# Log-distances from one product per head, and ScalarE writing two of four heads in the cross-attention

## The reference, cut to what matters

```python
log_fg = jax.nn.log_sigmoid(f_pre)
lf_cs = jnp.cumsum(log_fg, axis=-1)
...
log_d = lf[..., 1:, None] - lf[..., None, 1:] + i_pre[..., None, :]
log_d = jnp.where(mask, log_d, -jnp.inf)
m = jnp.max(log_d, axis=-1, keepdims=True)
d_mat = jnp.exp(log_d - m)
scores = jnp.einsum('bhtd,bhsd->bhts', q, k) * (1.0 / np.sqrt(DH))
s_mat = scores * d_mat
denom = jnp.maximum(jnp.abs(jnp.sum(s_mat, axis=-1, keepdims=True)), jnp.exp(-m)) + BACKEND_EPS
return jnp.einsum('bhts,bhsd->bhtd', s_mat, v) / denom
```

```python
def stablemax(x):
    s = jnp.where(x >= 0, x + 1.0, 1.0 / (1.0 - x))
    return s / jnp.sum(s, axis=-1, keepdims=True)
```

## Time and profile before

| what | value |
|---|---|
| median of three runs | 3640.21 us |
| profiled execution, its own time | 3634.66 us |
| span of its records | 3633.0 us |
| PE busy over the span | 2876.1 us (79%) |
| DVE busy | 2268.1 us (62%) |
| ACT busy | 1511.0 us (42%) |
| POOL busy | 667.5 us (18%) |

### The profile page before, as it was taken

One profiled execution on the slowest core, in us unless ns is written; L12 is line 12 of the kernel. 1 busy time (PEld: TensorE's weight loads), 2 busy tenths in 40 slices (PEclk: granted clock), 3 DMA queues, 4 the chain that ended last, 5 costly groups with the idle time before them and its releaser, 6 DMA issues. The chain is left out here.

```text
span 3633.0 us, 60719 instructions
## 1 busy us (share of the span) xinstructions
PE 2876.1 (79%) x21702; PEld 2244.0 (62%) x21703; DVE 2268.1 (62%) x3977; ACT 1511.0 (42%) x2470; POOL 667.5 (18%) x640
## 2 busy tenths in 40 slices
PE   4999877777655699999206999879999999177796
PEld 3666555555445588888205888756666666166686
DVE  5554557777644211111456888879999999778542
ACT  1233244434311122222004666568888888178000
POOL 0111103333346201001570000021111110000600
PEclk9999988888855799999658999889999999699898
DMA  3000051111132444444230000000000000034444
GB/s 110 0 0 0 20 205 53 53 53 53 36 123 96 151 145 141 145 142 141 86 102 27 1 1 1 1 31 13 13 13 13 13 13 7 25 162 185 173 150 162
DMA packets 109948, 259.90 MB, mean 72 GB/s; under 512 B 15040, under 2 KB 52928, under 8 KB 101056
## 3 DMA queue, kind: packets, MB, share of 16 engines
q1 hardware_dynamic: 91712, 204.85, 16.4%
q0 software_dynamic: 18048, 52.45, 4.4%
HBM read 169.17 MB, written 88.08 MB: 71 GB/s over the span
## 5 line engine op out<-in xcount | busy, mean ns | idle before, releaser
L1765 DVE TENSOR_SCALAR e_low<-bank 128x2048 f32<-128x2048 f32 x128 | 293.1, 2290 | 37.1 <-PE bank L1637 34.0
L1159 ACT ACTIVATE cx_h<-bank,c_b 128x256 f32<-128x256 f32 x288 | 120.7, 470 | 409.6 <-PE bank L1114 409.6
L1114 PE MATMUL bank<-cx_zT,cx_w 128*128 128x256 f32 x1152 | 262.5, 381 | 1.8 <-DMA cx_w<-cw_dram 0.9
L1125 PE MATMUL bank<-c_w,cx_h 128*128 x1152 | 260.4, 379 | 0.0
L1589 ACT ACTIVATE e_low<-e_low 128x2048 f32<-128x2048 f32 x128 | 245.1, 1915 | 2.1
L1586 ACT ACTIVATE e_low<-e_low 128x2048 f32<-128x2048 f32 x128 | 243.5, 1903 | 0.0
L1114 PEld LDWEIGHTS bank<-cx_zT,cx_w 128*128 128x128 f32 x1152 | 220.3, 191 | 32.3 <-DMA cx_w<-cw_dram 1.3
L2131 PE MATMUL bank<-f_wout,fd_q 128*128 128x256 f32 x1024 | 224.2, 383 | 19.6 <-DVE fd_q L2150 19.6
L1125 PEld LDWEIGHTS bank<-c_w,cx_h 128*128 128x128 f32 x1152 | 213.6, 190 | 25.9
L2131 PEld LDWEIGHTS bank<-f_wout,fd_q 128*128 128x128 f32 x1024 | 196.7, 192 | 46.9 <-DVE fd_q L2150 19.8
L1766 DVE TENSOR_SCALAR e_high<-bank 128x1536 f32<-128x1536 f32 x128 | 223.8, 1749 | 0.0
(11 more groups left out here) (362 smaller groups left out, 6781.9 us busy)
## 6 DMA issues: line engine op xcount, KB each, us to landing
cx_w<-cw_dram SPq DMA_DIRECT2D x72, 512.0 KB, 3.2
hidden<-fu_h SPq DMA_DIRECT2D x32, 1024.0 KB, 3.9
fd_h<-hidden SPq DMA_DIRECT2D x32, 1024.0 KB, 4.8
cx_rows<-expert_rows SPq DMA_DIRECT2D x72, 256.0 KB, 3.2
slot_y<-cx_y POOLq DMA_DIRECT2D x72, 256.0 KB, 2.5
X<-x_dram SPq DMA_DIRECT2D x4, 2048.0 KB, 16.0
g_cT<-ctxT_dram SPq DMA_DIRECT2D x32, 256.0 KB, 5.4
queries<-g_qT SPq DMA_DIRECT2D x32, 256.0 KB, 6.2
```

The lines of the kernel that those rows point to most:

```text
L1114: last = nc.tensor.matmul(H[k][f // 2][:, (f % 2) * GROUP_ROWS:(f % 2 + 1) * GROUP_ROWS], w1[k][:, c, f * P:(f + 1) * P], zT[k][:, c, :], ...
L1125: last = nc.tensor.matmul(Y[k][:, n * D:(n + 1) * D], h[k][:, f, n * P:(n + 1) * P], w2[:, bass.ds(e, 1), f, :].rearrange("p o d -> p (o d ...
L1159: nc.scalar.activation(h[k][:, f, :], H[k][f // 2][:, (f % 2) * GROUP_ROWS:(f % 2 + 1) * GROUP_ROWS], ACT.Gelu, bias=b1[:, bass.ds(e, 1), ...
L1765: nc.vector.tensor_scalar(flat(low[n % RING][:]), HEADS4.rearrange("p r s -> p (r s)"), -1.0, 0.0, ALU.mult, ALU.max).then_inc(neg_ready, 1)
```

## The change

**Recurrent attention.** The log-distance g[s] - top[t] is taken apart. g[s] is constant over a row of the tile (sources lie on the partitions), so it no longer goes through the product: PE turns gg once a group (own_term), ACT copies it to gT, and the exponential takes it as its bias. Since the bias differs between the two halves of the sources, the exponential of a head is two instructions, of 256 and of 128 columns. -top[t] comes from one product: a constant bf16 table minus of -1 in a head's three rows, filled in the gate stage by four copies, times top3, which holds the three bf16 parts of top. The mask stays a product. lefts and rights go, and part 1 and part 2 of prepare change. The three column blocks are now stored so that the first 256 columns are the first half of the sources and the last 128 the second half; scores and values keep their column counts.

**Cross-attention.** DVE writes high of heads 0 and 1, ACT of heads 2 and 3.

```diff
-LEFT1, LEFT1C, LEFT2, LEFT2C = (4 + 4 * k for k in range(4))
-RIGHT1, RIGHT1C, RIGHT2, RIGHT2C = (20 + 8 * k for k in range(4))
...
-            table = lambda at, n: s["rows"][:, at:at + n]
-            nc.vector.tensor_copy(table(BLOCK01, 2), ends[:])
-            nc.vector.tensor_tensor(table(EVEN, 1), low[:, 0:1], high[:, 0:1], ALU.add)
-            nc.vector.scalar_tensor_tensor(table(ODD, 1), low[:, 1:2], -1.0, high[:, 1:2], ALU.mult, ALU.subtract)
-            nc.vector.tensor_scalar(table(LEFT1, LANES4), lane[:], ends[:, 0:1], None, ALU.mult)
-            nc.vector.tensor_scalar(table(LEFT1C, LANES4), lane[:], ends[:, 1:2], -1.0, ALU.mult, ALU.mult)
-            nc.vector.tensor_scalar(table(LEFT2, LANES4), lane[:], low[:, 0:1], None, ALU.mult)
-            nc.vector.tensor_scalar(table(LEFT2C, LANES4), lane[:], high[:, 0:1], -1.0, ALU.mult, ALU.mult)
-            nc.vector.tensor_tensor(table(RIGHT1, HEADS), high[:, 2:2 + HEADS], high[:, 2 + HEADS:2 + 2 * HEADS], ALU.add)
...
+            nc.vector.tensor_copy(s["part"][:, 0:1], low[:, 0:1])
+            nc.vector.tensor_scalar(s["part"][:, 1:2], low[:, 1:2], -1.0, None, ALU.mult)
+            nc.vector.tensor_copy(s["part"][:, 2:3], high[:, 0:1])
+            nc.vector.tensor_tensor(heads[:], low[:, 2:2 + HEADS], low[:, 2 + HEADS:2 + 2 * HEADS], ALU.add).then_inc(rows_ready, 1)
+            dve.wait_ge(rows_ready, 1)
+            nc.vector.tensor_tensor(heads[:], heads[:], high[:, 2 + HEADS:2 + 2 * HEADS], ALU.add).then_inc(rows_ready, 1)
+            dve.wait_ge(rows_ready, 2)
+            for j in LANES:
+                nc.vector.tensor_scalar(which[:, j, :], heads[:], lane[:, j:j + 1], -1.0, ALU.mult, ALU.mult).then_inc(rows_ready, 1)
...
+                if g < LANES4:
+                    nc.vector.tensor_copy(s["minus"][:, g], which[:, g, :, None].to_broadcast([P, HEADS, P]))
...
         soft, cum, gg, top, gm = (sb(n, [P, S]) for n in ("soft", "cum", "gg", "top", "gm"))
-        x0, x, rest = (sb(n, [P, S]) for n in ("x0", "x", "rest"))
-        hi, mid, lo, y0, both = (sb(n, [P, S], BF) for n in ("hi", "mid", "lo", "y0", "both"))
-        left = [sb(f"left{k}", [P, LANES4, S], BF) for k in range(2)]
-        right = [sb(f"right{k}", [P, HEADS, S], BF) for k in range(2)]
+        rest, y0, y1 = (sb(n, [P, S]) for n in ("rest", "y0", "y1"))
+        hi, mid, lo = (sb(n, [P, S], BF) for n in ("hi", "mid", "lo"))
+        top3 = [sb(f"top3{k}", [P, COLS], BF) for k in range(2)]
...
-                nc.scalar.activation(decay[r][:], DD[r % 2][:, 0:COLS], ACT.Exp).then_inc(decay_ready, 1)
+                g, j, h = q // 8, q // 2 % LANES4, QUAD * (q % 2) + r
+                if q % 8 == 0 and r == 0:
+                    act.wait_ge(gT_ready, g + 1)
+                own = lambda n: gT[g % 2][:, n, j, h:h + 1]
+                nc.scalar.activation(decay[r][:, 0:S], DD[r % 2][:, 0:S], ACT.Exp, bias=own(0))
+                nc.scalar.activation(decay[r][:, late], DD[r % 2][:, late], ACT.Exp, bias=own(1)).then_inc(decay_ready, 1)
...
+                turned = b % LANES4 == 2 and b // LANES4 + 1 < GROUPS
...
+                if turned:
+                    act.wait_ge(gT_raw, b // LANES4 + 2)
...
+                if turned:
+                    nc.scalar.activation(gT[(b // LANES4 + 1) % 2][:], by_lane(DEN[:, S:2 * S]), ACT.Copy).then_inc(gT_ready, 1)
...
+            act.wait_ge(gT_raw, 1)
+            nc.scalar.activation(gT[0][:], by_lane(DEN[:, S:2 * S]), ACT.Copy).then_inc(gT_ready, 1)
...
-                pe.wait_ge(left_ready, 2 * (LANES4 * (b // LANES4) + j + 1))
-                pe.wait_ge(right_ready, 2 * (HEADS * (b // LANES4) + h + 1))
-                for part in range(2):
-                    nc.tensor.matmul(wide(out), left[part][:, j, 0:P], right[part][:, h, :].rearrange("p (x y) -> p x y", x=2), start=part == 0, stop=False)
-                for part in range(2):
-                    nc.tensor.matmul(out[:, P:S], left[part][:, j, P:S], right[part][:, h, P:S], start=False, stop=False)
-                nc.tensor.matmul(out[:, 0:S], t["identb"][:], t["maskneg"][:], start=False, stop=True).then_inc(dd_raw, 1)
+                pe.wait_ge(top3_ready, b // LANES4 + 1)
+                nc.tensor.matmul(out[:, 0:COLS], minus[:, j, h, :], top3[b // LANES4 % 2][:], start=True, stop=False)
+                nc.tensor.matmul(wide(out), t["identb"][:], t["maskneg"][:].rearrange("p (x y) -> p x y", x=2), start=False, stop=True).then_inc(dd_raw, 1)
...
-                    nc.tensor.matmul(wide(SC[r]), key[part, c, 0:P], query[part, c, :].rearrange("p (x y) -> p x y", x=2), start=True, stop=True)
+                    nc.tensor.matmul(SC[r][:, 0:S], key[part, c, 0:P], query[part, c, :], start=True, stop=True)
...
-                    nc.tensor.matmul(SC[r][:, P:S], key[part, c, P:S], query[part, c, P:S], start=True, stop=True).then_inc(sc_raw, 1)
+                    nc.tensor.matmul(SC[r][:, late], key[part, c, P:S], query[part, c, P:S], start=True, stop=True).then_inc(sc_raw, 1)
...
-                        x = wide(sm[c][r]) if n == 0 else sm[c][r][:, P:S]
+                        x = sm[c][r][:, 0:S] if n == 0 else sm[c][r][:, late]
...
+                if c and b % LANES4 == 2 and b // LANES4 + 1 < GROUPS:
+                    own_term(b // LANES4 + 1)
                 if c and b % LANES4 == 0:
                     pe.wait_ge(chain, PREP * (b // LANES4) + 4)
+                    pe.wait_ge(gT_ready, b // LANES4 + 1)
...
+            def own_term(g):
+                pe.wait_ge(chain, PREP * g + 2)
+                if g:
+                    pe.wait_ge(em0, g)
+                for n in range(TB):
+                    last = nc.tensor.transpose(DEN[:, S + n * P:S + (n + 1) * P], gg[:, n * P:(n + 1) * P], t["ident"][:])
+                last.then_inc(gT_raw, 1)
...
+            own_term(0)
...
+                    if g:
+                        dve.wait_ge(gT_raw, g)
...
                 if part == 1:
-                    ch.did(nc.vector.tensor_scalar(x0[:], gg[:], col(BLOCK01), None, ALU.mult)).see()
-                    ch.did(nc.vector.scalar_tensor_tensor(x[:], top[:], col(BLOCK23), x0[:], ALU.mult, ALU.add)).see()
-                    ch.did(nc.vector.tensor_copy(hi[:], x[:])).see()
+                    ch.did(nc.vector.tensor_copy(hi[:], top[:])).see()
+                    ch.did(nc.vector.tensor_tensor(rest[:], top[:], hi[:], ALU.subtract)).see()
+                    ch.did(nc.vector.tensor_copy(mid[:], rest[:])).see()
                 if part == 2:
-                    ch.did(nc.vector.tensor_tensor(rest[:], x[:], hi[:], ALU.subtract)).see()
-                    ch.did(nc.vector.tensor_copy(mid[:], rest[:])).see()
-                    ch.did(nc.vector.tensor_scalar(y0[:], hi[:], col(EVEN), None, ALU.mult))
-                    if g:
-                        dve.wait_ge(right_ready, 2 * HEADS * g)
-                        dve.wait_ge(left_ready, 2 * LANES4 * g)
-                    ch.did(nc.vector.tensor_tensor(lo[:], rest[:], mid[:], ALU.subtract)).see()
-                    ch.did(nc.vector.scalar_tensor_tensor(both[:], mid[:], col(ODD), y0[:], ALU.mult, ALU.add))
-
-            def lefts(g, lanes):
...
-                for j in lanes:
...
-                    for part, x in enumerate((both, lo)):
-                        a, k = ((LEFT1, LEFT1C), (LEFT2, LEFT2C))[part]
-                        nc.vector.tensor_scalar(left[part][:, j, :], x[:], col(a + j), col(k + j), ALU.mult, ALU.add).then_inc(left_ready, 1)
-
-            def rights(g, c):
...
-                for h in range(QUAD * c, QUAD * (c + 1)):
-                    for part, x in enumerate((both, lo)):
-                        a, k = ((RIGHT1, RIGHT1C), (RIGHT2, RIGHT2C))[part]
-                        nc.vector.tensor_scalar(right[part][:, h, :], x[:], col(a + h), col(k + h), ALU.mult, ALU.add).then_inc(right_ready, 1)
+                    ch.did(nc.vector.tensor_tensor(lo[:], rest[:], mid[:], ALU.subtract))
+                    ch.did(nc.vector.tensor_scalar(y0[:], hi[:], part_col(0), None, ALU.mult)).see()
+                    ch.did(nc.vector.scalar_tensor_tensor(y1[:], mid[:], part_col(1), y0[:], ALU.mult, ALU.add)).see()
+                    if g > 1:
+                        dve.wait_ge(dd_raw, 8 * QUAD * (g - 1))
+                    nc.vector.scalar_tensor_tensor(top3[g % 2][:, 0:S], lo[:], part_col(2), y1[:], ALU.mult, ALU.add)
+                    nc.vector.scalar_tensor_tensor(top3[g % 2][:, late], lo[:, P:S], part_col(2), y1[:, P:S], ALU.mult, ALU.add).then_inc(top3_ready, 1)
...
-            lefts(0, range(LANES4))
-            rights(0, 0)
-            rights(0, 1)
...
-                    if g and k == 0:
-                        rights(g, 1)
-                        lefts(g, (3,))
-                    if g + 1 < GROUPS and k == 6:
-                        lefts(g + 1, range(3))
-                    if g + 1 < GROUPS and k == 7:
-                        rights(g + 1, 0)
...
```

(6 more changed lines are left out.)

50 lines of the change are left out of this document (22 added, 28 removed).

## The result

The changed kernel takes 3585.7 us (median of 4 runs, 3581.7 to 3587.7), the kernel before 3639.9 on the same chip: a ratio of 0.9852, 95% interval 0.9835 to 0.9869. That is 54 us less, where 68 were forecast; the time lies inside the range and 0.3 us inside the upper end of the forecast's own range (3586), which is luck: four runs spread over 6 us.

The account below looks back on a forecast made before the run. Bounds: a chain round all engines in the recurrent attention, PE in the cross-attention. Recurrent -65.5 us (-27.5 - 36 - 3 + 1) and cross-attention -2.5 give -68, a median of 3572 us, range 3535 to 3600 (own 3556 to 3586).

Parts of the forecast that it names:

- Products, -0.96 an entry: Recurrent chain: one product per head, 640 columns instead of 1024, shortens each of 32 batches by 0.96 us.
- ACT, +0.05 twice an entry: Recurrent chain: splitting each exponential in two adds 0.05 us twice a batch; upper bound +0.16 a head, without any overlap.
- Tables, -36 us: Recurrent attention: DVE's left and right table instructions before the weighing go, saving 36 us over 7 groups (30 to 42).
- (a): Rival, 16%: PE's clock stays high in half of the recurrent batches, 19 to 37 us more saved, total 3544.
- Opening, -3 us: Start of the recurrent attention: the first group's 24 table instructions go, saving 3 us, bounds 0 and 10.
- Preparation, 0: Recurrent attention: preparing the next group on DVE changes by 0, with 4 us either way.
- Gate stage, +1 us: Gate stage: four copies of the table minus, 1.2 us each; the first delays the second group's tiles by 1 us.
- Cross-attention, -2.5 us: Cross-attention: PE loses 0.78 us waiting for zT and gains 0.86 elsewhere, -0.08 a batch, -2.5 us.
- The loop through zT: Cross-attention: ACT copies zT later, so PE's keys start 7.33 us after the scores of the step before, not 6.55.
- (b): Rival, 12%: in cross-attention the copy of zT isn't binding, which saves up to 27 us, total 3547.
- (c): Rival, 14%: ACT is dearer, +11 us in cross-attention and +9 for the recurrent split exponentials, total 3592.
- (d): Rival, 4%: PE's clock falls for good in the recurrent stage, +49 us, total 3685, slower than before.

## Why the prediction was right, and where its terms were off

- **What bounds the stages.** Right for both. No engine fills the recurrent stage and its length follows the chain; the cross-attention follows PE and what PE waits for, and ends at PE's own 21.37 us an entry once the waits are gone.
- **Products, -0.96 an entry.** The instructions are as forecast (1.22 us for heads 2 and 3 at the low level with the switch to values, before 1.81; at the high level heads start 0.38 us apart or less, before 0.45). The term gives 21 us, not 30.7. What was off is that "values take 1.44 here" stood as a constant: values got 0.23 us an entry longer with the shorter products, 7 us in all. The idle time ahead of the turn back got 0.19 longer too, and why is not traced.
- **ACT, +0.05 twice an entry.** This is the mis-sized term that costs most. It is +0.05 for the split, as argued, and +0.59 an entry for the bias, which the forecast never priced, though the sum of the earlier trace rows was only of instructions without one. The trace of before had the price: in its gate stage, a Tanh of 256 columns out of PSUM with a bias lasts 0.47 us, a copy without one 0.38:

```profile
458.31 0.47 ACT L521 ACTIVATE b_pre<-bank,g_bias 128x256 f32<-128x256 f32 x1 [1.08 <-PE bank L496]
```

```profile
764.77 0.38 ACT L612 ACTIVATE b_oT<-bank 128x256 f32<-128x256 f32 x1
```

  The upper bound, "+0.16 without any overlap", was therefore no bound: measured from the same instructions it is 0.472 + 0.367 - 0.49 = 0.35 us a head.
- **Tables, -36 us.** Right in sign and place, too small: 47.2, without the opening. Most of what is above the forecast is in the entry with ten table instructions (4.44 a group for 2.7). The forecast had taken 1.12 us off its price there, because its values ran at the low level; without the tables they run at the high one, so this time went with the tables. Rival (a) had this as its mechanism.
- **Opening, -3 us.** Right: from softplus to the first product 9.1 us before, 6.3 after.
- **Preparation, 0.** Right, between 0 and the 4 us that were given as a bound: the last part is 3.16 us (697.91 to 701.07) instead of 2.58, 0.6 a group, with DVE's instructions at 0.90 and 1.12 under POOL's work. The first part is 2.33 instead of 2.88: its scan, 1.24 in the earlier trace rows, takes 0.68 in all groups after, but in the second execution of the kernel before it does so in five groups of the seven too.
- **Gate stage, +1 us.** The four copies take 0.69 us each, not 1.2, and the tiles of the second and third group come 0.6 and 1.2 us later. By the means of all executions the stage is 0.7 longer; the rest of the +3 is there without the edit too.
- **Cross-attention, -2.5 us.** Each instruction and the place of the new wait were right; the term gave -8.3. An inner entry falls from 22.17 to 21.93, -0.24 where -0.08 was forecast; that is 7.7 us in 32 entries, and the first entries of the stage bring the rest. The loop through zT was priced at +7.33 and is +7.22, and PE waits 0.66 us an entry for it: 0.11 of the 0.16 an entry by which the term was off. The other 0.05 is not traced.
- **Rivals.** (b) needs zT not to bind: wrong, moving the copy is worth 9.5 us more. (c) came true in part, by a price on ACT, but that of the recurrent stage and of another cause. (d) did not come: 0.84 became 0.87. (a) came in one entry of four: in the six inner groups the entry behind an idle time of 1.70 us kept the high level through its values six times of six (11.48 us an entry), and the three others had their values at the low level, 18 times of 18.

The sum by measured terms: -21.0 for the products, -47.2 for the tables, -2.8 for the opening, +2.7 for the split and 0 to +4 for the preparation make -68 to -64, where the kernel without the bias has -66.5. With the bias, +18.8, the stage has -47.7, and with the cross-attention, -8.3, it is -56; the gate and feed-forward stages move by the few us that lie between this and the two medians. That the time came within 0.4% of the forecast owes much to errors of opposite sign: +18.8 for the bias and +9.7 for the products against -11.2 for the tables and -5.8 for the cross-attention.

## What to carry to other kernels

Before an instruction is given one more operand, look in the trace for the same engine's instruction with that operand, anywhere in the program: here a bias was 0.09 us of a 0.37 to 0.47 us instruction and cost 19 us. Where a stage has several waits close behind one another, work out the next two limits at once: the change gained 8 us in the cross-attention, and two moves of existing lines made it 25 without any work removed. Work that was taken away right behind an idle time of PE gave less than its length here, since the steps behind it ran at the low clock for longer: 0.23 us came back of 0.87. And before a count in one trace is taken as an effect, count it in a second execution of the same kernel: it was 18 of 30 in one and 22 in the other here.
